# Reordering the preparation, the end of the self attention and the feed-forward weight splits of a one-core transformer block

## The chip, the core and the metric

The kernel runs on one core of a Trainium2 chip. A core has five engines with a queue each: TensorE (PE, with PEld for its weight loads), VectorE (DVE), ScalarE (ACT), GpSimd (POOL) and SyncE (SP), which here only issues DMAs. They share the on-chip memory SBUF; TensorE writes only to the eight PSUM banks. The metric is the device time of one execution in microseconds (us), the median of several runs.

## The reference

One transformer block, float32: for each of 4 batches 1024 rows of width 256, and a context of 64 rows of width 192. Sixteen heads of width 64, feed-forward width 1024.

```python
h = _ln(x, g1, be1)
x = _attn(h, h, Wq1, Wk1, Wv1, Wo1, bo1) + x          # self attention, 1024 keys
h = _ln(x, g2, be2)
x = _attn(h, context, Wq2, Wk2, Wv2, Wo2, bo2) + x    # cross attention, 64 keys
h = _ln(x, g3, be3)
y = h @ Wp + bp
a, gate = (y[..., :FF_HID], y[..., FF_HID:])
x = a * jax.nn.gelu(gate, approximate=False) @ W2 + b2 + x
```

## The kernel before

Every engine has its own function, and each is one straight program: the order of the work is the order in which the Python loops write it, and semaphores tie the engines together. A matmul operand is split into a high part and a rest (`hi`, `lo`, "split" below), and three products of parts stand for one.

**Preparation.** The context is turned and multiplied with `Wk2` and `Wv2` in 16 products (`context_product`, banks S0a, S0b, S1a, S1b, PV, PJ in turn, copied to `kv2` by DVE for even and by ACT for odd numbers). `turn_wq2` transposes `Wq2` in 16 tiles into two banks, from which ACT makes four copies to `wq2T`. DVE takes the statistics of the first batch (`stats1`), ACT the root (`ln_root`, with the load of an activation table), DVE the inverse (`ln_inverse`) and the rows `xn` of one half of the batch (`norm1`, four TENSOR_SCALAR, L684). `turn_norm` transposes `xn` (L324) through banks T0 and T1 into `hT`. `fold_keys` multiplies `wq2T` with `kv2` (L382), four times for each half of the batch. Then the query and key projections of the first head pair follow (`project_qk`, L411). POOL meanwhile splits `Wq1`, `Wk1` and `Wv1` (`split_weights`: a TENSOR_SCALAR at L1224, a TENSOR_TENSOR at L1226) and adds a bias.

**Self attention.** 64 groups C: 8 head pairs by 2 halves of queries by 4 batches. In each, TensorE makes the scores of 8 key tiles (L463, L467), ACT the exponentials, TensorE the product with the values (`attend`, L480) and the sum over the keys (`sum_keys`, L491). POOL adds up the exponentials (`add_probs`, L1273). ACT copies the sums, DVE inverts them (`invert_sums`, L782), POOL multiplies (`scale_oT`, L1279), and `out1` (L501) is the output product of a tile. For the next group DVE takes row maxima and makes `shift` (L775), without which the scores can't be finished. In the last group DVE also splits the folded keys of the cross attention (`split_keys`, L807, tile `crossA`), which `score2` needs.

**Cross attention.** A pipeline of 32 rounds i, one for each row tile: `turn2(i-2)` (transposes of the probabilities, L546), `score2(i)` (L532), `turn_half` for the next norm (in rounds with i % 4 of 2 or 3), `out2(i-3)` (L562), and in the first eight rounds `out1` of the last batch. DVE takes the inverse of each softmax sum (L817), POOL multiplies with it (`scale2`, L1284). In rounds with i % 4 of 0 or 1 DVE also makes rows `xn` (`norm2`, L684). POOL splits cross keys (L1290), cross values (L1297) and the feed-forward weights (`split_ffn`, eight pieces: `Wp` quarters, 128x1024, at even numbers and `W2` quarters, 128x512, at odd ones).

**Feed-forward.** L576 up, L590 down; the outputs are stored by SP in eight pieces of four row tiles (L1476).

Of the kernel before, what the change touches and what calls it, by code (L numbers as in the profile page):

```python
# [48 lines left out]
def block_kernel(nc, x, ctx, Wq1, Wk1, Wv1, Wo1, bo1, Wq2, Wk2, Wv2, Wo2, bo2, Wp, bp, W2, b2,  # L49
# [32 lines left out]
    with stack:  # L82
# [222 lines left out]

        def v_slot(D, jt):
            return jt

        @block.tensor
        def _(e):  # L310
# [50 lines left out]
            def turn_wq2():  # L361
                for k in range(KT):
                    for h in range(PAIRS // 4):
                        bank = f"T{(2 * k + h) % 2}"
# [233 lines left out]
            turn_wq2()  # L598
            for c in range(CHUNKS):
                turn_norm((1, c))  # L600
                for p in range(PAIRS // 2):
                    fold_keys(PAIRS // 2 * c + p)
# [26 lines left out]
            for i in range(NT + 3):  # L629
# [10 lines left out]
                if i < TILES:  # L640
                    out1(B - 1, i, ("PJ", "PV")[i % 2])
# [14 lines left out]
        def _(e):  # L656
# [122 lines left out]
            def invert_sums(C):  # L779
                need.wait_ge(s.sum_copied, C + 1)  # L780
                need.wait_ge(s.oT_scaled, C)
                e.reciprocal(inv[:, :], sums[:, :]).then_inc(s.sum_inverse, 1)  # L782
# [95 lines left out]
            for n in range(2 * PAIRS):  # L878
                context_product(n)
                if n >= PAIRS:  # L880
                    stats1(0, n - PAIRS)
            ln_inverse(rs1[:, :], (1, 0))
            for c in range(CHUNKS):
                norm1(c)
                turn_norm((1, c))
                for p in range(PAIRS // 2):
# [12 lines left out]
            for C in range(NC):  # L899
                b, n = divmod(C, BC)  # L900
                if C + 1 < NC:
# [3 lines left out]
                    gather_max(C + 1)  # L905
                if C >= 2:
                    invert_sums(C - 2)
                if b + 1 < B and 5 <= n < 5 + TILES // 2:
# [9 lines left out]
                if C == NC - 1:  # L918
                    for k in range(KT):
                        split_keys(k, 0)  # L920
                        split_keys(k, 1)
                    invert_sums(C - 1)
                whole_array(slot(C))
            for i in range(NT + 3):
# [10 lines left out]
                if i < TILES:  # L935
                    out1(B - 1, i, ("PJ", "PV")[i % 2])
                if i == 2:
                    invert_sums(NC - 1)
# [26 lines left out]
        def _(e):  # L965
# [69 lines left out]
            def turn_wq2():  # L1035
                for k in range(KT):
                    for h in range(PAIRS // 4):
                        need.wait_ge(s.wq2_turned, 2 * k + h + 1)
                        e.copy(wq2T[:, 4 * h:4 * h + 4, k * PART:(k + 1) * PART],
                               banks[f"T{(2 * k + h) % 2}"].rearrange("p (j n) -> p j n", j=4)).then_inc(s.wq2T_in, 1)  # L1040
# [52 lines left out]
            def copy_sums(C, bank="PJ"):  # L1093
                need.wait_ge(s.summed, C + 1)
                need.wait_ge(s.sum_inverse, C)
# [60 lines left out]
            ln_root(mv1[:, :, 1], (1, 0), (1, TILES - 1))  # L1156
            turn_wq2()
            for c in range(CHUNKS):
                turn_norm((1, c))
                for p in range(PAIRS // 2):  # L1160
# [58 lines left out]
        def _(e):  # L1219
# [55 lines left out]
            def scale_oT(C):  # L1275
                there = oT[:, C // CHUNKS % PRING, C % CHUNKS * BANK:(C % CHUNKS + 1) * BANK]
                need.wait_ge(s.sum_inverse, C + 1)
# [31 lines left out]

            e.memset(ident[:, :], 0.0).then_inc(s.const, 1)  # L1310
# [32 lines left out]
            for i in range(NT + 3):  # L1343
# [13 lines left out]
                if i >= TILES + 4 and i % 2 == 0 and i // 2 - TILES // 2 - 2 < 8:  # L1357
                    split_ffn(i // 2 - TILES // 2 - 2)
# [4 lines left out]
        def _(e):  # L1363
# [109 lines left out]
            for i in range(NCH):  # L1473
                b, t0 = ORDER[FORDER[i] // CHUNKS], FORDER[i] % CHUNKS * TPC
                need.wait_ge(s.y_added, TPC * (i + 1))
                e.dma_start(out[b, t0 * PART:(t0 + TPC) * PART, :].rearrange("(t p) d -> p t d", p=PART),  # L1476
                            xf[:, i % 4]).then_inc(s.y_stored, 16)
# [7 lines left out]
            need.wait_ge(s.y_stored, 16 * NCH)  # L1485
# [23 lines left out]
```

## Time and profile before

| | |
|---|---|
| median of 3 runs | 2096.39 us (2095.53 to 2096.85) |
| the profiled execution | 2095.88 us |
| its span, first to last instruction | 2094.0 us |
| TensorE matmul busy | 2060.5 us, 98% |
| VectorE / ScalarE / GpSimd busy | 1403.2 / 1044.5 / 1414.8 us |
| mean granted TensorE clock | 0.998 |

The chain of work that ended last is TensorE for 94% of the span. Preparation takes the first 60 us, self attention goes to about 1555, cross attention to about 1813, feed-forward to the end. In a row of the timeline, the bracket at the end says how long the engine was idle before the instruction and what ended that wait.

### The profile page before, as it was taken

How to read it: one execution, taken by the hardware profiler on the slowest of the kernel's cores; microseconds unless marked ns; L12 is line 12 of the kernel's file. 1: busy time of each engine (PE TensorE's matmuls, PEld its weight loads, DVE VectorE, ACT ScalarE, POOL GpSimd, SP SyncE). 2: the span in 40 equal slices, each digit the busy share in tenths (PEclk: the TensorE clock that was granted, in tenths of full speed). 3: DMA queues.
4: the chain of work that ended last, by engine and by line, in shares of the span. 5: the costliest groups of instructions: out<-in, count | busy, mean ns of one | idle time of the engine just before them, and what ended most of it. 6: DMA issues, size and time to landing. Idle time of an engine off the chain costs nothing.

```text
span 2094.0 us, 31744 instructions
## 1 busy us (share of the span) xinstructions
PE 2060.5 (98%) x12500; PEld 1401.7 (67%) x12500; DVE 1403.2 (67%) x2139; ACT 1044.5 (50%) x1644; POOL 1414.8 (68%) x745
## 2 busy tenths in 40 slices
PE   7999999999999999999999999999998999999999
PEld 5656656567556556666656666565557989888888
DVE  5667677754766875568678566757866899755453
ACT  3445456542545564345456433545655666543332
POOL 2499799975997997779799767978885577200000
PEclk9999999999999999999999999999999999999999
DMA  6400000000100000010000001000011420000100
GB/s 192 151 6 21 6 6 16 6 6 21 41 6 6 21 6 6 1 61 6 6 6 21 6 1 46 11 6 1 21 24 38 141 81 1 1 21 21 41 11 31
DMA packets 46070, 58.74 MB, mean 28 GB/s; under 512 B 5857, under 2 KB 40289, under 8 KB 44769
## 3 DMA queue, kind: packets, MB, share of 16 engines
q1 hardware_dynamic: 45920, 56.71, 8.6%
q8 instruction: 99, 1.62, 0.3%
q14 instruction: 51, 0.41, 0.1%
HBM read 38.88 MB, written 17.83 MB: 27 GB/s over the span
## 4 chain that ended last, share of the span: by engine, by line
PE 94%; DVE 2%; POOL 1%; ACT 1%; issue 1%; DMA 0%; SPq 0%; POOLq 0%; DVEq 0%; ACTq 0%
PE score L480 21%; PE score L463 17%; PE score L576 9%; PE score L467 5%; PE attn_project L590 4%; PE score L411 4%; PE attn_project L562 4%; PE score L532 4%; PE attn_project L411 4%; PE first_score L437 3%; PE attn_project L501 3%; PE score L423 3%; PE first_score L491 3%; PE attn_project L437 2%; PE score L501 2%; PE attn_project L423 1%
## 5 line engine op out<-in xcount | busy, mean ns | idle before, releaser
L1273 POOL TENSOR_TENSOR acc<-acc,pT 128x1024 f32<-128x1024 f32 x384 | 913.7, 2380 | 55.1 <-POOL acc L1273 0.4
L1080 ACT ACTIVATE pT<-score 128x1024 f32<-128x1024 f32 x512 | 524.8, 1027 | 103.9 <-PE score L467 62.0
L463 PE MATMUL score<-qk 64*128 64x512 f32 x3072 | 459.8, 399 | 4.6 <-ACT pT L1080 2.8
L480 PE MATMUL score<-pT,vT 128*64 128x512 f32 x2016 | 446.5, 595 | 0.0
L760 DVE TENSOR_REDUCE nmax<-first_score 128x1 f32<-128x512 f32 x512 | 348.3, 680 | 12.5 <-PE first_score L437 9.2
L760 DVE TENSOR_REDUCE nmax<-attn_project 128x1 f32<-128x512 f32 x512 | 347.2, 678 | 0.0
L463 PEld LDWEIGHTS score<-qk 64*128 64x128 f32 x3072 | 258.1, 184 | 126.7 <-ACT pT L1080 70.8
L480 PEld LDWEIGHTS score<-pT,vT 128*64 128x64 f32 x2016 | 139.2, 137 | 274.5 <-issue 251.8
L1270 POOL TENSOR_TENSOR acc<-pT 128x1024 f32<-128x1024 f32 x64 | 153.6, 2400 | 187.4 <-ACT pT L1080 187.4
L782 DVE RECIPROCAL inv<-sums 128x512 f32<-128x512 f32 x64 | 214.0, 3345 | 4.8 <-POOL oT L1279 4.8
L1091 ACT COPY oT<-score 128x512 f32<-128x512 f32 x63 | 36.9, 586 | 356.9 <-PE score L480 356.9
L467 PE MATMUL score<-shift,pick 64*128 64x512 f32 x1024 | 207.0, 391 | 0.0
L437 PE MATMUL first_score<-qk 64*128 64x512 f32 x512 | 200.3, 391 | 0.0
L437 PE MATMUL attn_project<-qk 64*128 64x512 f32 x512 | 200.0, 391 | 0.0
L576 PE MATMUL score<-hT,wp 128*128 128x512 f32 x768 | 183.9, 395 | 0.0
L775 DVE TENSOR_TENSOR shift<-first_score,mask 128x512 fp32r<-128x512 f32 x64 | 44.2, 691 | 191.1 <-PE first_score L447 191.1
L576 PEld LDWEIGHTS score<-hT,wp 128*128 128x128 f32 x768 | 142.4, 188 | 32.1
L1260 POOL TENSOR_TENSOR xres<-xres,rows 128x1024 f32<-128x1024 f32 x8 | 19.2, 2401 | 205.1 <-DVE xn L684 205.1
L754 DVE SCALAR_TENSOR_TENSOR qk<-score,qk 128x512 fp32r<-128x512 f32 x67 | 46.2, 690 | 153.7 <-ACT qk L1061 153.7
L1284 POOL TENSOR_TENSOR probs<-probs,rsum 128x1024 f32<-128x1024 f32 x32 | 60.9, 1905 | 90.2 <-DVE rsum L817 90.2
L467 PEld LDWEIGHTS score<-shift,pick 64*128 64x128 f32 x1024 | 100.3, 184 | 21.9 <-DVE shift L775 0.7
L1061 ACT ACTIVATE qk<-score 128x512 fp32r<-128x512 f32 x67 | 40.1, 598 | 145.1 <-PE score L411 145.1
(159 smaller groups left out, 3050.3 us busy)
## 6 DMA issues: line engine op xcount, KB each, us to landing
xres<-x_middle SPq DMA_DIRECT2D x10, 512.0 KB, 4.1
xres<-in_x SPq DMA_DIRECT2D x4, 1024.0 KB, 7.0
raw_qk<-in_L_xattn_Wq SPq DMA_DIRECT2D x32, 128.0 KB, 2.2
raw_qk<-in_L_xattn_Wk SPq DMA_DIRECT2D x32, 128.0 KB, 2.3
raw_v<-in_L_xattn_Wv SPq DMA_DIRECT2D x8, 512.0 KB, 4.1
keys_all<-keys SPq DMA_DIRECT2D x1, 4096.0 KB, 11.8
values_all<-values SPq DMA_DIRECT2D x1, 4096.0 KB, 12.4
out_x<-xres SPq DMA_DIRECT2D x8, 512.0 KB, 2.9
```

Of the source, the lines that this page charges most:

```text
L411: last = e.matmul(banks[bank], wqk[:, P % 2, w, kind, k, :], hT[:, h, k, c * BANK:(c + 1) * BANK], start=(i == k == 0), stop=(i == 2 and k ...
L437: last = e.matmul(banks[bank], qk[P % 2][r, w, q0:q0 + PART], qk[P % 2][r, 2 + h, half * BANK:(half + 1) * BANK], start=(m == 0), stop=(m ...
L463: e.matmul(bank, qk[P % 2][r, 2 + h, keys], qk[P % 2][r, w, queries], start=(part == 0), stop=False)
L467: e.matmul(bank, pick[r, :], shift[r, :], start=False, stop=True).then_inc(s.scored, 1)
L480: last = e.matmul(banks[bank][head * DH:(head + 1) * DH, :], vT[:, v_slot(D, jt), c0:c0 + DH], pT[:, jt, head, :], start=(jt == 0), stop=( ...
L501: last = e.matmul(banks[bank][:, 0:DIM], oT[:, (PAIRS * b + p) % PRING, t * PART:(t + 1) * PART], wo1[:, p, :], start=(p == 0), stop=(p == ...
L576: last = e.matmul(banks[bank], wp[q][:, w, k, which, o:o + PART], hT[:, h, k, (c % 2) * BANK:(c % 2 + 1) * BANK], start=(term == k == 0), ...
L760: e.tensor_reduce(nmax[:, head, t, half:half + 1], banks[PASS_BANKS[head][half]], AX.X, ALU.max, negate=True).then_inc(s.row_max, 1)
L782: e.reciprocal(inv[:, :], sums[:, :]).then_inc(s.sum_inverse, 1)
L1080: e.activation(pT[:, jt].rearrange("p h n -> p (h n)"), SC[R % 2][:, :], ACT.Exp).then_inc(s.exponential, 1)
L1270: e.tensor_tensor(total, pT[:, jt - 1], pT[:, jt], ALU.add).then_inc(s.probs_added, 1)
L1273: e.tensor_tensor(total, total, pT[:, jt], ALU.add).then_inc(s.probs_added, 1)
```

## The change

Six edits.

1. Preparation. TensorE turns the first half of the first norm before `Wq2`, not after; `Wq2` now goes through PV and PJ, not T0 and T1. DVE takes the statistics after context products 2 to 9, not 8 to 15. ACT makes the root after product 11, and its copies of `Wq2` stand behind the first half of the norm. DVE makes the rows of the second half before its copies of the first four folds.
2. The four key splits: one moves to the group before the last, two ahead of the inverse at the last group's start, one stays between the last two inverses.
3. The very last inverse is made in two halves, after rounds 1 and 2; `sum_inverse` counts two for each group.
4. `out1` of tile 2 goes to PV instead of PJ.
5. The eight feed-forward splits stand in rounds 14, 15, 16, 22, 23, 24, 30, 31 instead of 12, 14, ... 26.
6. The last four row tiles are stored one by one.

```diff
+        def last_out1(i):
+            return ("PJ", "PV")[(i + (i == 2)) % 2]
...
-            turn_wq2()
             for c in range(CHUNKS):
                 turn_norm((1, c))
+                if c == 0:
+                    turn_wq2()
...
-                    out1(B - 1, i, ("PJ", "PV")[i % 2])
+                    out1(B - 1, i, last_out1(i))
...
-            def invert_sums(C):
+            def invert_sums(C, halves=(0, 1)):
+                part = slice(halves[0] * BANK // 2, (halves[-1] + 1) * BANK // 2)
...
-                if n >= PAIRS:
-                    stats1(0, n - PAIRS)
+                if 2 <= n < 2 + TILES:
+                    stats1(0, n - 2)
             ln_inverse(rs1[:, :], (1, 0))
+            norm1(0)
             for c in range(CHUNKS):
-                norm1(c)
                 turn_norm((1, c))
+                if c == 0:
+                    norm1(1)
...
+                if C == NC - 1:
+                    split_keys(0, 1)
+                    split_keys(1, 0)
                 if C >= 2:
                     invert_sums(C - 2)
+                if C == NC - 2:
+                    split_keys(0, 0)
...
-                    for k in range(KT):
-                        split_keys(k, 0)
-                        split_keys(k, 1)
+                    split_keys(1, 1)
                     invert_sums(C - 1)
...
-                if i == 2:
-                    invert_sums(NC - 1)
+                if i in (1, 2):
+                    invert_sums(NC - 1, (i - 1,))
...
-            ln_root(mv1[:, :, 1], (1, 0), (1, TILES - 1))
-            turn_wq2()
+                if n == TILES + 3:
+                    ln_root(mv1[:, :, 1], (1, 0), (1, TILES - 1))
...
+            FFN_SPLITS = [i for i in range(TILES + 6, NT) if i % TILES in (6, 7, 0)]
...
-                if i >= TILES + 4 and i % 2 == 0 and i // 2 - TILES // 2 - 2 < 8:
-                    split_ffn(i // 2 - TILES // 2 - 2)
+                if i in FFN_SPLITS:
+                    split_ffn(FFN_SPLITS.index(i))
...
-                need.wait_ge(s.y_added, TPC * (i + 1))
-                e.dma_start(out[b, t0 * PART:(t0 + TPC) * PART, :].rearrange("(t p) d -> p t d", p=PART),
-                            xf[:, i % 4]).then_inc(s.y_stored, 16)
+                pieces = [slice(0, TPC)] if i + 1 < NCH else [slice(j, j + 1) for j in range(TPC)]
+                for part in pieces:
+                    need.wait_ge(s.y_added, TPC * i + part.stop)
```

The order of instructions shows the places. Rows are instructions in their engine's order, with the line of the kernel they stand in.

TensorE in the preparation, from the last context products (`ctxT,wkv`) to the first fold (`kv,wq2T`), of before:

```order
L356 MATMUL score<-ctxT,wkv 128x256 x8
L369 MATMUL first_score<-ident,wq 128x128 x16
L324 MATMUL first_score<-ident,xn 128x128 x8
L382 MATMUL score<-kv,wq2T 128x256 x8
L382 MATMUL attn_project<-kv,wq2T 128x256 x4
```

and of the change:

```order
L360 MATMUL score<-ctxT,wkv 128x256 x8
L328 MATMUL first_score<-ident,xn 128x128 x8
L373 MATMUL attn_project<-ident,wq 128x128 x16
L386 MATMUL score<-kv,wq2T 128x256 x8
L386 MATMUL attn_project<-kv,wq2T 128x256 x4
```

The 16 transposes of `Wq2` moved from ahead of the 8 transposes of `xn` to between them and the folds.

VectorE at the end of the self attention, from the last gathering of maxima to the first `score2` maximum (`nmax<-score`), of before:

```order
L767 TENSOR_REDUCE maxima<-nmax 128x2x4
L782 RECIPROCAL inv<-sums 128x512
L775 TENSOR_TENSOR shift<-first_score,mask 128x512
L782 RECIPROCAL inv<-sums 128x512
L807 TENSOR_TENSOR crossA<-crossA 128x512 x4
L782 RECIPROCAL inv<-sums 128x512
L827 TENSOR_REDUCE nmax<-score 128x16
```

and of the change:

```order
L772 TENSOR_REDUCE maxima<-nmax 128x2x4
L788 RECIPROCAL inv<-sums 128x512
L813 TENSOR_TENSOR crossA<-crossA 128x512
L780 TENSOR_TENSOR shift<-first_score,mask 128x512
L813 TENSOR_TENSOR crossA<-crossA 128x512 x2
L788 RECIPROCAL inv<-sums 128x512
L813 TENSOR_TENSOR crossA<-crossA 128x512
L788 RECIPROCAL inv<-sums 128x512
L833 TENSOR_REDUCE nmax<-score 128x16
```

Three of the four splits moved ahead of the second inverse, one of them ahead of the last `shift`.

GpSimd in rounds 12 to 16 of the cross attention (`probs` is `scale2`, `wp` and `w` are the feed-forward splits), of before:

```order
L1290 TENSOR_TENSOR crossA<-crossA 128x512 x2
L1224 TENSOR_SCALAR wp<-wp_in 128x1024
L1226 TENSOR_TENSOR wp<-wp_in,wp 128x1024
L1284 TENSOR_TENSOR probs<-probs,rsum 128x1024
L1290 TENSOR_TENSOR crossA<-crossA 128x512 x2
L1284 TENSOR_TENSOR probs<-probs,rsum 128x1024
L1254 TENSOR_TENSOR xres<-xres,rows 128x256 x2
L1224 TENSOR_SCALAR w<-w_in 128x512
L1226 TENSOR_TENSOR w<-w_in,w 128x512
```

and of the change:

```order
L1303 TENSOR_TENSOR crossA<-crossA 128x512 x2
L1297 TENSOR_TENSOR probs<-probs,rsum 128x1024
L1303 TENSOR_TENSOR crossA<-crossA 128x512 x2
L1297 TENSOR_TENSOR probs<-probs,rsum 128x1024
L1267 TENSOR_TENSOR xres<-xres,rows 128x256 x2
L1237 TENSOR_SCALAR wp<-wp_in 128x1024
L1239 TENSOR_TENSOR wp<-wp_in,wp 128x1024
L1297 TENSOR_TENSOR probs<-probs,rsum 128x1024
L1267 TENSOR_TENSOR xres<-xres,rows 128x256 x2
L1237 TENSOR_SCALAR w<-w_in 128x512
L1239 TENSOR_TENSOR w<-w_in,w 128x512
```

The `wp` split left round 12, which also holds a split of cross keys, for round 14; the `w` split went from round 14 to 15.

## Rows read from the trace of the kernel before

**Rows 1.** The page: busy time of the engines.

```profile
PE 2060.5 (98%) x12500; PEld 1401.7 (67%) x12500; DVE 1403.2 (67%) x2139; ACT 1044.5 (50%) x1644; POOL 1414.8 (68%) x745
```

**Rows 2.** Waits of TensorE: us in total, times, longest.

```profile
PE attn_project L501 <- DVE hT L714: 4.7, 2, 2.4
...
PE first_score L546 <- POOL probs L1284: 1.8, 2, 1.3
...
PE attn_project L501 <- POOL oT L1279: 1.5, 1, 1.5
...
PE score L532 <- DVE crossA L807: 1.1, 1, 1.1
```

**Rows 3.** Timeline, preparation: start, duration, engine, line, tiles, count, [idle before].

```profile
22.68 0.42 DVE L732 COPY kv<-score 128x256 f32<-128x256 f32 x1 [0.23 <-PE score L356]
...
23.34 1.04 POOL L1224 TENSOR_SCALAR wv<-raw_v 128x1024 fp32r<-128x1024 f32 x1 [3.65 <-DMA raw_v<-in_L_xattn_Wv]
...
25.43 1.05 ACT L1039 COPY wq2T<-first_score 128x512 f32<-128x512 f32 x2
...
25.80 3.59 DVE L684 TENSOR_SCALAR xn<-xres,mv,rs 128x256 f32<-128x256 f32 x4
...
27.65 1.26 POOL L1226 TENSOR_TENSOR wqk<-raw_qk,wqk 128x512 fp32r<-128x512 f32 x1
...
29.44 1.97 PE L324 MATMUL first_score<-ident,xn 128*128 128x128 f32 x8 [2.25 <-DVE xn L684]
...
30.60 0.78 ACT L1020 ACTIVATE hT<-first_score,cols 128x512 fp32r<-128x512 f32 x1 [2.78 <-PE first_score L324]
...
31.34 3.79 PE L382 MATMUL score<-kv,wq2T 64*128 64x256 f32 x16
...
37.54 1.37 DVE L684 TENSOR_SCALAR xn<-xres,mv,rs 128x256 f32<-128x256 f32 x4
...
38.97 1.10 PE L324 MATMUL first_score<-ident,xn 128*128 128x128 f32 x8 [2.09 <-DVE xn L684]
...
45.44 5.83 PE L411 MATMUL score<-hT,wqk 128*128 128x512 f32 x24 [0.15 <-DVE keys L738]
```

**Rows 4.** DMA issues, first 20 us: KB each, us from issue to landing.

```profile
xres<-in_x SPq DMA_DIRECT2D x1, 1024.0 KB, 8.2
```

**Rows 5.** Windows: us, busy time per engine, then the granted clock.

```profile
34.00:35.00 1.00, 1.00 (x8) 0.76 (x6) 1.00 (x2) 0.06 (x1) 0.00 (x0) 0.50 0.00 0
35.00:36.00 1.00, 1.00 (x12) 0.90 (x10) 0.72 (x2) 0.60 (x1) 0.00 (x0) 0.97 0.00 0
```

**Rows 6.** Timeline, end of the self attention.

```profile
1538.41 0.69 DVE L775 TENSOR_TENSOR shift<-first_score,mask 128x512 fp32r<-128x512 f32 x1 [3.21 <-PE first_score L447]
...
1543.91 3.35 DVE L782 RECIPROCAL inv<-sums 128x512 f32<-128x512 f32 x1 [4.80 <-POOL oT L1279]
...
1547.18 9.28 DVE L807 TENSOR_TENSOR crossA<-crossA 128x512 fp32r<-128x512 f32 x4
...
1561.11 3.72 PE L501 MATMUL attn_project<-wo,oT 128*128 128x256 f32 x16 [1.48 <-POOL oT L1279]
```

**Rows 7.** Timeline, TensorE, round 3 of the cross attention.

```profile
1592.59 3.72 PE L501 MATMUL attn_project<-wo,oT 128*128 128x256 f32 x16 [2.28 <-DVE hT L714]
```

**Rows 8.** Timeline, rounds 12 to 16 of the cross attention.

```profile
1671.79 3.58 DVE L684 TENSOR_SCALAR xn<-xres,mv,rs 128x256 f32<-128x256 f32 x2
...
1672.82 2.40 POOL L1226 TENSOR_TENSOR wp<-wp_in,wp 128x1024 fp32r<-128x1024 f32 x1
...
1689.01 1.90 POOL L1284 TENSOR_TENSOR probs<-probs,rsum 128x1024 f32<-128x1024 f32 x1 [0.95 <-DVE rsum L817]
...
1692.55 1.03 PE L546 MATMUL first_score<-ident,probs 128*128 128x128 f32 x8
```

**Rows 9.** The page, DMA issues over the span.

```profile
raw_qk<-in_L_xattn_Wq SPq DMA_DIRECT2D x32, 128.0 KB, 2.2
...
out_x<-xres SPq DMA_DIRECT2D x8, 512.0 KB, 2.9
```

More of the change, by code:

```diff
@@ L363, in turn_wq2 @@
                     for h in range(PAIRS // 4):
-                        bank = f"T{(2 * k + h) % 2}"
+                        bank = ("PV", "PJ")[h]
                         need.wait_ge(s.wq2_loaded, 16)
@@ L777, in make_shift @@
                                 mask[:, :].unsqueeze(2).to_broadcast([PART, TPC, PART]), ALU.mult).then_inc(s.shift_in, 1)
-            def invert_sums(C):
+            def invert_sums(C, halves=(0, 1)):
+                part = slice(halves[0] * BANK // 2, (halves[-1] + 1) * BANK // 2)
                 need.wait_ge(s.sum_copied, C + 1)
                 need.wait_ge(s.oT_scaled, C)
-                e.reciprocal(inv[:, :], sums[:, :]).then_inc(s.sum_inverse, 1)
+                e.reciprocal(inv[:, part], sums[:, part]).then_inc(s.sum_inverse, len(halves))
             def out1(b, t, bank="PJ"):
@@ L935, in _ @@
                 if i < TILES:
-                    out1(B - 1, i, ("PJ", "PV")[i % 2])
-                if i == 2:
-                    invert_sums(NC - 1)
+                    out1(B - 1, i, last_out1(i))
+                if i in (1, 2):
+                    invert_sums(NC - 1, (i - 1,))
                 if i in (TPC + 1, 2 * TPC + 1):
@@ L1039, in turn_wq2 @@
                         e.copy(wq2T[:, 4 * h:4 * h + 4, k * PART:(k + 1) * PART],
-                               banks[f"T{(2 * k + h) % 2}"].rearrange("p (j n) -> p j n", j=4)).then_inc(s.wq2T_in, 1)
+                               banks[("PV", "PJ")[h]].rearrange("p (j n) -> p j n", j=4)).then_inc(s.wq2T_in, 1)
             def fold_keys(p):
@@ L1094, in copy_sums @@
                 need.wait_ge(s.summed, C + 1)
-                need.wait_ge(s.sum_inverse, C)
+                need.wait_ge(s.sum_inverse, 2 * C)
                 e.copy(sums[:, :], banks[bank]).then_inc(s.sum_copied, 1)
@@ L1155, in _ @@
                 context_product(n)
-            ln_root(mv1[:, :, 1], (1, 0), (1, TILES - 1))
-            turn_wq2()
+                if n == TILES + 3:
+                    ln_root(mv1[:, :, 1], (1, 0), (1, TILES - 1))
             for c in range(CHUNKS):
                 turn_norm((1, c))
+                if c == 0:
+                    turn_wq2()
                 for p in range(PAIRS // 2):
@@ L1276, in scale_oT @@
                 there = oT[:, C // CHUNKS % PRING, C % CHUNKS * BANK:(C % CHUNKS + 1) * BANK]
-                need.wait_ge(s.sum_inverse, C + 1)
+                need.wait_ge(s.sum_inverse, 2 * (C + 1))
                 need.wait_ge(s.oT_written, C + 1)
@@ L1474, in _ @@
                 b, t0 = ORDER[FORDER[i] // CHUNKS], FORDER[i] % CHUNKS * TPC
-                need.wait_ge(s.y_added, TPC * (i + 1))
-                e.dma_start(out[b, t0 * PART:(t0 + TPC) * PART, :].rearrange("(t p) d -> p t d", p=PART),
-                            xf[:, i % 4]).then_inc(s.y_stored, 16)
+                pieces = [slice(0, TPC)] if i + 1 < NCH else [slice(j, j + 1) for j in range(TPC)]
+                for part in pieces:
+                    need.wait_ge(s.y_added, TPC * i + part.stop)
+                    e.dma_start(out[b, (t0 + part.start) * PART:(t0 + part.stop) * PART, :].rearrange(
+                        "(t p) d -> p t d", p=PART), xf[:, i % 4, part]).then_inc(s.y_stored, 16)
                 if i + 4 < NCH:
@@ L1484, in _ @@
             need.wait_ge(s.x2_stored, 16 * NCH // 2)
-            need.wait_ge(s.y_stored, 16 * NCH)
+            need.wait_ge(s.y_stored, 16 * (NCH + TPC - 1))
 _NAMES = ["x", "ctx_768"] + ["L0_xattn_" + n for n in (
```

## The prediction

> **What bounds the kernel now.** The page first: TensorE is busy for 2060.5 us of the 2094.0 us span [rows 1], so without taking matmuls away at most 33.5 us can be won, and the change takes none away. What counts is where TensorE stands still. The waits of TensorE come next. Of its named waits, four can be touched by the edits: 4.7 us for `hT` ahead of two `out1` tiles, 1.8 us for `probs` ahead of two `turn2`, 1.5 us for the scaled `oT` ahead of the first `out1`, 1.1 us for the key splits ahead of the first `score2` [rows 2]. Then the timeline of each of these places, to see what was late and what is late next. The preparation has further waits and also a low clock. At the very end no engine works and a store lands. Everything behind a stall of TensorE here moves as a block, since TensorE is the bound between these places; so a saving at one place should reach the end.
>
> **Preparation (edit 1).** Before, DVE is done with its context copies at 23.10 (22.68 + 0.42), then needs the root, and begins `xn` at 25.80 [rows 3]. `x` lands 8.2 us after an issue early in the stage [rows 4], so statistics between the copies hold up no copy, and the root is ready before the last copy. With about 0.25 us for the inverse `xn` can begin at 23.4, 2.4 us sooner. But the four rows took 3.59 us there, against 1.37 us for the second half [rows 3]. The difference is POOL: its four splits (`wv`, then `wqk`, two instructions each) run from 23.34, the landing of `wv`, to 28.91 (27.65 + 1.26), and `xn` ended at 29.39, just behind them. Four rows and four POOL instructions in a row: if one DVE row gets in between two POOL instructions, as the 3.58 us of the two `xn` rows against the 2.40 us `wp` split also look [rows 8], then the rows that start at 23.4, just behind `wv`'s start, are done with the last split, at 29.1. The gain is 0.3 us, not 2.4.
>
> The Trainium skill speaks against the earlier norm in the same way: SBUF — State Buffer, "Who interferes with whom", says that VectorE and GpSimd share one port pair, held by whichever starts first for its whole instruction, and that a `tensor_scalar` can be such an instruction. By that rule moving the rows earlier, into the splits, wins nearly nothing; without it the step would be worth 2.4 us and more. Here only the rows' durations bear it out.
>
> Then the path grows. Before, the `Wq2` transposes ran while DVE made `xn`; now they stand between the norm's transposes and the folds. TensorE has by then been idle for over 5 us, and restarts at the low clock: before, the granted clock was 0.50 (1.2 GHz) at 34 to 35 us and 0.97 in the next, 5.6 us after the restart at 29.44 [rows 5]. From 29.1: 8 transposes 1.97 us, to 31.1; 16 more at that rate 3.9 us. ACT first makes three activations of some 0.78 us, begun 1.16 us behind the first transpose as before, so to 32.6, and copies each quarter of `Wq2` in 0.53 us (1.05 for two) [rows 3]. Two banks hold two quarters, the third waits for the first copy (33.1), the fourth ends at 35.1, its copy at 35.6. The four folds, at the full clock again, take 32 instructions of 0.12 us (estimate: half of 3.79/16), to 39.4. The second half's rows are long there, and its transposes start at 39.4 instead of 38.97; from there to the projection at 45.44 it is the same 6.47 us. **Sum: +0.4 us.** Bounds: with no POOL in the way the rows end at 24.8, the clock stays high, and the same path ends 5.8 us sooner than before; with rows at 29.4 and the low clock through the folds (0.24 each) it is 4.6 later. If DVE's first row wins the race at 23.34 against POOL, the rows end with the third split (27.65) and the path is 2 us shorter.
>
> **End of the self attention (edits 2 to 4).** The four splits took 9.28 us, 2.32 each, from 1547.18 [rows 6], and `score2` waited 1.1 us for them [rows 2]. The inverse behind them made `out1` wait another 1.48 us [rows 6]. Now one split stands ahead of `shift`, where DVE sat idle 3.21 us: 2.32 fits. Two stand where it sat 4.80 us (1539.1 to 1543.9): 4.64 fits. The inverse (3.35), the last split (2.32) and the last inverse (3.35) then end near 1553, or 1555 if POOL comes late because DVE now gets in between its sums. TensorE needs the keys at 1555.5 and the scaled `oT` at 1558.5, and the scaling takes POOL about 1.3 us behind a sum. Both waits go: -1.1 and -1.5 us.
>
> `out1` of tile 2 waited 2.4 us for the rest of `hT`, since both used PJ [rows 2]. On PV it only needs `out1` of tile 1 added, which is long done: -2.4. In round 3 the half norm goes to PV, behind this tile's add, which DVE has made by then; `out1` of tile 3 waited 2.28 us there [rows 7] for DVE, which was late because of the whole inverse of 3.35 us in round 2. One half is now in round 1, where DVE waits for ACT's copy of the sums and delays the softmax sum by some 2 us; POOL's product for it is still done 2.7 us before `turn2(1)` by my count. So round 2 has 1.7 us less on DVE, of which 1.1 us reaches `out1`. **Sum: -1.1 - 1.5 - 2.4 - 1.1 = -6.1 us**, between -3 (only the first two, and a little) and -7.5.
>
> **Feed-forward splits (edit 5).** In round 12 the second `xn` row stood behind the `wp` split, 3.58 us for two rows, and `turn2` came 1.3 us late; in round 20 the same cost 0.5 [rows 2, 8]. Both rounds lose the split: -1.8 us. What is late next: rounds 14 and 23 now hold a product (1.9), a bias and a `wp` split (3.5), about 6.8 us of POOL in a round of 7.0. The product of the next round starts some 0.6 us late; before it ended at 1690.91 and `turn2` read it at 1692.55 [rows 8], 1.6 us of slack. Rounds 14, 15, 22 and 23 have no `xn` rows to block. In round 30 the split meets `norm3`, which delays DVE by 1.4 us; the last products have over 2 us. **-1.8 us**, between 0 and -1.8.
>
> **Stores (edit 6).** The last store of 512 KB took 2.9 us to land; a piece of 128 KB takes 2.2 (loads, the nearest row) [rows 9]. The other three leave while TensorE works. **-0.7 us**, between 0 and -1.
>
> **Sum** +0.4 - 6.1 - 1.8 - 0.7 = -8.2 us. The profiled execution took 2095.88 us, the median of the runs is 0.5 us above it. 2095.88 - 8.2 = 2087.7.
>
> **Rivals.** What a measurement of this kernel can tell from no change is 0.2%, 4.2 us.
> (a) The forecast, the late stages win and the preparation gives about nothing: 2087.7, own range 2085 to 2090. 55%.
> (b) The preparation wins too, as DVE's rows get ahead of POOL (the start at 23.4 against 23.34 is a tossed coin): 2 us or up to 5.8 us less than before instead of 0.4 more, 2081.5 to 2085.3. 25%.
> (c) The preparation costs: `Wq2` on the path at the low clock and the folds low too, +2 to +4.6: 2089.3 to 2091.9. 12%. For it speaks the longer idle of TensorE, against it that the clock rose 5.6 us after the restart.
> (d) The moves do nothing at the end of the self attention, because POOL, not DVE, is late: POOL's sums slip by each DVE instruction that gets in, and the scaled `oT` comes when it came before. Then only 2.4 + 1.8 + 0.7 are won: 2091 to 2093. 5%.
> (e) Slower: the POOL port. If each of the eight moved splits stalled `turn2` as that of round 12 did, 1.3 us each, that costs 10.4 us where nothing is won by edit 5: 2095.88 + 0.4 - 6.1 - 0.7 + 10.4 = 2099.9. It turns the sign from 0.8 us for a split on (6.4/8). Against it: eight rounds before held a split, and two waited. 3%.
>
> **How the numbers follow.** Faster by over 0.2% (below 2092.2) in (a), (b), (c) and half of (d): 0.93, less something for what I have overlooked, 0.88. Within 0.2%: 0.08. Slower: 0.04. The range goes from 2083 to 2091.5: it leaves out the far end of (b) and the ends of (c) and all beyond.
>
> **What would show it.** After: `xn` rows of the first half ending near 29 (b: near 27.7 or before), the first projection at about 45.5, a granted clock of 0.5 between; no wait of `score2` for `crossA`, none of the first `out1` for `oT`, one wait of `out1` for `hT` of about 1 us instead of 4.7 in two; no waits of L546 for `probs`; the last store 2.2 us to landing. The prediction is wrong if the first projection moves by more than 3 us, if the first splits hold up `shift`, or if new waits for `probs` appear in rounds 15, 24 or 32.

## The result, and the profile after

The changed kernel took 2082.8 us (median of 6 runs, 2082.07 to 2085.07) against 2096.39 us before (2095.53 to 2098.53): 0.9936 of the time, interval 0.9924 to 0.9949, 13.6 us less. The forecast was 2087.7, with a range from 2083.0 to 2091.5: the sign was right, the gain was 5 us larger, and the median lies 0.2 us below the range. In two later sets of runs the same kernel had medians of 2085.2 and 2084.84; why it moves so much is part of what follows.

Busy time, from the page of the changed kernel (against [rows 1]):

```profile
PE 2058.4 (99%) x12500; PEld 1400.2 (67%) x12500; DVE 1399.6 (67%) x2140; ACT 1044.2 (50%) x1644; POOL 1415.0 (68%) x745
```

The span is 2080.5 us, 13.5 less, at the same matmuls. Waits of TensorE from 1552 us, where the last attend ends, to the feed-forward part, changed kernel (against [rows 2]; total, times, longest), all that there are:

```profile
PE attn_project L566 <- ACT turned L1150: 0.8, 1, 0.8
PE first_score L550 <- ACT sums L1107: 0.8, 1, 0.8
PE attn_project L505 <- DVE hT L719: 0.7, 1, 0.7
```

No wait for `crossA`, `oT` or `probs`; of 4.7 us for `hT` 0.7 is left. Timeline of the changed kernel, preparation (against [rows 3]):

```profile
21.52 0.42 DVE L737 COPY kv<-score 128x256 f32<-128x256 f32 x1 [1.30 <-PE score L360]
...
22.09 4.26 DVE L689 TENSOR_SCALAR xn<-xres,mv,rs 128x256 f32<-128x256 f32 x4
...
22.73 1.04 POOL L1237 TENSOR_SCALAR wv<-raw_v 128x1024 fp32r<-128x1024 f32 x1 [3.80 <-DMA raw_v<-in_L_xattn_Wv]
...
23.86 2.34 POOL L1239 TENSOR_TENSOR wv<-raw_v,wv 128x1024 fp32r<-128x1024 f32 x1
...
26.41 1.25 PE L328 MATMUL first_score<-ident,xn 128*128 128x128 f32 x8 [4.06 <-DVE xn L689]
...
27.45 1.92 PE L373 MATMUL attn_project<-ident,wq 128*128 128x128 f32 x8
...
32.04 2.00 PE L386 MATMUL score<-kv,wq2T 64*128 64x256 f32 x16 [0.73 <-ACT wq2T L1050]
...
35.69 1.09 PE L328 MATMUL first_score<-ident,xn 128*128 128x128 f32 x8
...
42.16 4.19 PE L415 MATMUL score<-hT,wqk 128*128 128x512 f32 x17 [0.15 <-DVE keys L743]
```

The first projection stands at 42.16 instead of 45.44. The same view at the end of the self attention (against [rows 6, 7]):

```profile
1532.33 0.63 DVE L813 TENSOR_TENSOR crossA<-crossA 128x512 fp32r<-128x512 f32 x1
...
1536.19 4.87 DVE L813 TENSOR_TENSOR crossA<-crossA 128x512 fp32r<-128x512 f32 x2
...
1542.34 3.35 DVE L788 RECIPROCAL inv<-sums 128x512 f32<-128x512 f32 x1 [1.28 <-POOL oT L1292]
...
1545.61 2.01 DVE L813 TENSOR_TENSOR crossA<-crossA 128x512 fp32r<-128x512 f32 x1
...
1552.62 3.07 PE L536 MATMUL score<-crossA,hT 128*128 128x512 f32 x12
...
1555.53 3.61 PE L505 MATMUL attn_project<-wo,oT 128*128 128x256 f32 x16
...
1567.07 1.75 DVE L788 RECIPROCAL inv<-sums 128x256 f32<-128x256 f32 x1 [0.53 <-ACT sums L1107]
...
1582.58 3.72 PE L505 MATMUL attn_project<-wo,oT 128*128 128x256 f32 x16 [0.67 <-DVE hT L719]
```

With five landmarks of each trace the 13.5 us divide as follows:

| stretch | before | after | change | forecast |
|---|---|---|---|---|
| start to first projection | 45.44 | 42.16 | -3.28 | +0.4 |
| to the copy of the last attended heads | 1510.11 | 1510.58 | +0.47 | 0 |
| to the fourth `out1` | 37.04 | 29.84 | -7.20 | -6.1 |
| to the feed-forward part | 220.50 | 218.26 | -2.24 | -1.8 |
| to the last residual add | 277.11 | 277.11 | 0 | 0 |
| to the end of the span | 3.80 | 2.55 | -1.25 | -0.7 |

The landmarks of before are rows of [rows 3, 7], the others are in the same timelines. Most of the miss is in the first line of the table.

### The profile page after: what moved, and what is told of

The parts are those of the page before. It is cut to its first block, busy times and chain, and to the rows that moved or that the text cites. A ratio compares the mean times of both kernels' runs of the same rounds, so it can differ in the third digit from the quotient of the medians.

```text
span 2080.5 us, 31749 instructions
## 1 busy us (share of the span) xinstructions
PE 2058.4 (99%) x12500; PEld 1400.2 (67%) x12500; DVE 1399.6 (67%) x2140; ACT 1044.2 (50%) x1644; POOL 1415.0 (68%) x745
## 4 chain that ended last, share of the span: by engine, by line
PE 96%; DVE 2%; ACT 1%; issue 0%; DMA 0%; SPq 0%; DVEq 0%; ACTq 0%
PE score L484 21%; PE score L467 18%; PE score L580 9%; PE score L471 6%; PE attn_project L594 4%; PE attn_project L566 4%; PE score L536 4%; PE score L415 4%; PE first_score L441 4%; PE attn_project L415 4%; PE attn_project L505 3%; PE score L427 3%; PE first_score L495 3%; PE score L505 2%; PE attn_project L441 2%; PE attn_project L427 1%
## 5 line engine op out<-in xcount | busy, mean ns | idle before, releaser
L788 DVE RECIPROCAL inv<-sums 128x512 f32<-128x512 f32 (+1 forms) x65 | 214.7, 3303 | 3.7 <-POOL oT L1292 2.5
```

The lines of the kernel that those rows point to most:

```text
L788: e.reciprocal(inv[:, part], sums[:, part]).then_inc(s.sum_inverse, len(halves))
```

## The experiments

Ratios are to runs of the kernel before on the same chip. "Distance" below is from the start of VectorE's last `kv` copy (22.68 us before [rows 3]) to the first projection: it leaves out how early that copy comes. Its start moves between traces, from 22.52 to 23.80 us in five with the old order of the preparation and from 21.52 to 23.68 us in thirteen with the new one. TensorE's wait for the landing of `wkv` ahead of the first product is 1.4 to 3.4 us in these traces, so at least part of the scatter is that landing.

**The parts alone, and the kernel before once more.** e1: edit 1. e2: edits 2 to 4. e3: edits 5 and 6. e4: nothing changed.

> The kernel before with edit 1 alone (the preparation). Marks: start of the first projection, and the same counted from the start of the first copy of kv. Before: 45.44 and 35.57 us behind the first copy at 9.87; after the whole change: 42.16 and 33.57 behind 8.59. Theory A (landing and race): the edit itself is worth 2.0 us, because DVE gets three rows of xn in before POOL's first long instruction; the other 1.3 us is when the first weights land, which differs between executions. Then the second mark is 33.4 to 33.8, whatever the first copy's time, and the time is 2 to 3.5 us below before, ratio 0.9984 to 0.9990. Theory B (the prediction's working: one row for each POOL instruction, Wq2 on the path at the low clock): second mark 35.5 to 36.2, time as before or 0.4 us above. Theory C: the edit itself moves the first copy too, so all 3.3 us belong to it and the first copy is at 8.6 here.

> The kernel before with edits 2 to 4 alone (key splits, inverse in halves, bank of out1 tile 2). Mark: from the end of the last attend to the start of out1 of tile 3 (before 37.0 us, from 1555.55 to 1592.59; after the whole change 29.8). Theory A (the sum of four waits): 7.2 us fewer here, time 2088.5 to 2089.8. Theory B (part of that came from the shifted phase of POOL that the other edits bring): 5 us fewer or less, time above 2090.5.

> The kernel before with edits 5 and 6 alone (feed-forward splits, stores of the last rows). Marks: waits of turn2 for probs (before 1.3 and 0.5), and from the last add of the output to the end of the span (before 3.8; after 2.55). Theory A: both waits are gone and the tail is 1.25 us shorter, since a 128 KB store lands in 1.7 us and not in the 2.2 of the loads: in sum 3.0 us. Theory B: the waits went because of the other edits' phase shift, and one comes back here; 1.2 to 2.5 us in sum.

> The kernel before, unchanged, once more. Theory A (landing differs between executions): the first copy of kv starts anywhere from 8.5 to 10, and the first projection 35.6 us behind it, within 0.2. Theory C (the edit moved it): the first copy again at 9.87, within 0.1.

| run | us (runs) | beside before's | ratio, interval |
|---|---|---|---|
| e1 | 2095.81 (11) | 2096.12 (15) | 0.9995, 0.9986 to 1.0004 |
| e2 | 2088.6 (4) | 2096.12 | 0.9961, 0.9947 to 0.9974 |
| e3 | 2092.35 (1) | 2096.12 | one run |
| e4 | 2096.21 (1) | 2096.12 | one run |

e2 is worth 7.5 us and e3 3.8 in its single run (2.2 to the feed-forward part and 1.2 in the tail by its trace): theory A of both. e4 has VectorE's first `kv` copy at 8.70 us, which is theory A, but the first projection 37.3 us behind it, not 35.6: the stretch between the two scatters as well. In e1 the mark of theory A held (33.5 us) and its time did not: the trace had the first projection at 42.40, 3.0 us earlier than before, and the median stood still, in runs from 2091.25 to 2098.48. The mean granted clock of these runs goes with their time: 0.999 in the two fastest (2091.25, 2091.72), 0.998 in the next seven, 0.996 in the two slowest (2098.16, 2098.48). The trace tells where one such execution loses time. Windows of TensorE, e1 (us, busy, granted clock, DMA share, GB/s):

```profile
1574.00:1577.00 3.00, 0.55 (x3) 0.96 1.06 193
1577.00:1580.00 3.00, 3.00 (x9) 0.50 0.01 1
1580.00:1583.00 3.00, 3.00 (x19) 0.97 0.00 0
```

and the same place in the kernel before, 3 us later:

```profile
1577.00:1580.00 3.00, 0.55 (x4) 1.00 1.00 193
1580.00:1583.00 3.00, 3.00 (x16) 1.00 0.02 3
```

Both stand still for 2.45 us ahead of the third `out1`; in e1 the clock fell to 0.50 (1.2 GHz) for 3.4 us as the tile began, in the trace of before it did not. The cost is in the length of that tile (timeline, e1; 3.72 us in the kernel before):

```profile
1576.51 5.41 PE L501 MATMUL attn_project<-wo,oT 128*128 128x256 f32 x16 [2.45 <-DVE hT L715]
```

**e5: edits 1 to 4 together.** Does the preparation's gain arrive once the late waits are gone?

> Edits 1 to 4 together (preparation and end of self attention), the feed-forward splits and the stores as before. Edit 1 alone gave 2095.81 (-0.3) although its trace had the last attend 2.8 to 3 us earlier, and its clock fell to 1.2 GHz for 3.4 us at 1575 us of the span, inside the waits for the residual adds; edits 2 to 4 alone gave 2088.6 (-7.5). Theory A (the gain of edit 1 is real, 2.8 us, and was lost again to the clock in the waits at the end of self attention, which edits 2 to 4 take away): the two together give 2.8 + 7.5 = 10.3 us, 2085.8, no low clock outside the preparation, and a spread of the runs well under the 7 us of edit 1 alone. Theory B (edit 1 is worth what its own median says, the parts add up as measured): 0.3 + 7.5 = 7.8 us, 2088.3. Between them: 2087.

2087.86 us (5 runs, within 0.64) against 2095.89, ratio 0.9959 (0.9947 to 0.9972): 8.0 us less, near theory B. There was no late fall of the clock, and still edit 1 added only 0.5 us to the 7.5 of e2 (on another chip). The preparation of e5 says why, first the timeline, then windows of TensorE (us, busy, granted clock, DMA share, GB/s):

```profile
22.90 1.04 POOL L1237 TENSOR_SCALAR wv<-raw_v 128x1024 fp32r<-128x1024 f32 x1 [3.72 <-DMA raw_v<-in_L_xattn_Wv]
...
23.20 5.28 DVE L689 TENSOR_SCALAR xn<-xres,mv,rs 128x256 f32<-128x256 f32 x4
...
27.07 1.26 POOL L1239 TENSOR_TENSOR wqk<-raw_qk,wqk 128x512 fp32r<-128x512 f32 x1
```

```profile
26.00:28.00 2.00, 0.00 (x0) 0.55 1.12 324
28.00:30.00 2.00, 1.47 (x7) 0.50 0.49 25
30.00:32.00 2.00, 2.00 (x11) 0.50 0.00 0
32.00:34.00 2.00, 1.55 (x9) 0.75 0.00 0
```

GpSimd's split of `wv` began 0.3 us ahead of the first `xn` row, the four rows took 5.28 us, to just behind the end of the last split at 28.33, and the clock was low for 6.8 us. That is the forecast's own picture of this stage, with the first projection at 44.66. Which of the two engines starts first is called the race below.

**e6 to e8: two edits of the preparation in the changed kernel.** e6 puts the `Wq2` transposes ahead of the norm's again, on all engines that take part, e7 holds GpSimd back by one wait, e8 has both:

```diff
-            for c in range(CHUNKS):
-                turn_norm((1, c))
-                if c == 0:
-                    turn_wq2()
+            turn_wq2()
+            for c in range(CHUNKS):
+                turn_norm((1, c))
...
             split_wqk(0)
+            need.wait_ge(s.ln_rows, TPC)
             split_wv(0)
```

> The changed kernel, but with the Wq2 transposes ahead of the first norm's transposes again (their banks PV and PJ kept). In the trace of the changed kernel TensorE waits 4.06 us for xn (22.35 to 26.41), then does the Wq2 transposes (1.92 + 1.43 us) and waits 0.52 and 0.73 us for their copies; its clock is low from about 27 to 31 us. Theory A (the wait is only for xn, so 3.35 us of transposes fit into it): folds start at 28 instead of 32.04, VectorE's first fold copy then waits for its own xn rows (end 32.2) and not for TensorE, the first projection comes 1 us earlier through that, and 1.5 us more where the low clock is gone: 2080.3 to 2081.8. Theory B (the move of the transposes behind the norm is what won the preparation): the first projection comes 1 to 3 us later, 2084 to 2086.

> The changed kernel, but GpSimd's split of Wv waits for the first four xn rows of VectorE (one wait more on ln_rows). In the trace of the changed kernel these rows take 4.26 us (22.09 to 26.35) beside GpSimd's split, while the next four, with GpSimd idle, take 1.37 us. Theory A (the two engines hold each other up): the four rows take 1.4 us, end at 23.5, the transposes of the norm start at 23.6, and the first projection comes 2.8 us earlier, 39.3: 2080.0 (1.5 less still where the low clock goes too). GpSimd's splits then end 0.8 us later, which nothing waits for before the projection. Theory B (the rows are slow for another reason, as the DMA writes that land there): the rows take 4 us again and nothing is won, 2082.8 to 2083.6.

> Both of the last two edits in the changed kernel. TensorE does the Wq2 transposes from 22.35 to about 24.3 without a wait for xn (end 23.5), then the norm's from 24.3 and the second half of Wq2. Theory A: the idle 4.06 us are gone, the low clock of 3.4 us (1.7 us of work lost) with them, the first projection at 37.5 to 38.5 instead of 42.16: 2078 to 2079.5. Theory B (the chain through ScalarE and VectorE from the norm's transposes to the last fold copy, 15.8 us from 26.41 to 42.13, sets the projection, and only its start counts): as with GpSimd held alone, or later by the 1.9 us of Wq2 transposes that now stand ahead of the norm's where xn is early: 2080 to 2081.5.

| run | us (runs) | ratio, interval | `xn` rows | distance |
|---|---|---|---|---|
| e6 | 2082.27 (4) | 0.9931, 0.9917 to 0.9945 | 4.53 | 19.16 |
| e7 | 2079.95 (4) | 0.9922, 0.9907 to 0.9937 | 1.38 | 17.98 |
| e8 | 2082.66 (5) | 0.9933, 0.9921 to 0.9946 | 1.38 | 20.05 |

e7 came out as theory A had it (2080.0 forecast). Timeline, e7:

```profile
22.33 1.38 DVE L689 TENSOR_SCALAR xn<-xres,mv,rs 128x256 f32<-128x256 f32 x4
...
23.77 1.09 PE L328 MATMUL first_score<-ident,xn 128*128 128x128 f32 x8 [1.18 <-DVE xn L689]
...
23.80 1.04 POOL L1237 TENSOR_SCALAR wv<-raw_v 128x1024 fp32r<-128x1024 f32 x1 [4.82 <-DVE xn L689]
```

The clock stayed full throughout. In e8 my theory A (2078 to 2079.5) fell, and the time is above the range of theory B (2080 to 2081.5) too: TensorE filled the first gap with `Wq2` and the first folds, and then stood still for 4.4 us in one piece, because VectorE still had the second half's rows (3.11 us beside GpSimd) ahead of its first fold copy. The longest wait of TensorE up to 46 us, then windows, e8:

```profile
PE score L386 <- DVE keys L742: 4.4, 1, 4.4
```

```profile
30.00:32.00 2.00, 0.00 (x0) 1.00 0.00 0
32.00:34.00 2.00, 0.00 (x0) 0.76 0.00 0
34.00:36.00 2.00, 1.72 (x8) 0.50 0.00 0
```

The clock was low for 6.8 us and the gain of e7 was lost. In e6 the idle time was cut into waits of 2.1, 2.6 and 1.3 us and the clock never fell; but the rows were as long as ever. Its time lies between the two theories (2080.3 to 2081.8 and 2084 to 2086), nearer A: the full clock came, the earlier fold copies did not.

**e9 to e12: the changed kernel again, and edits 4, 3 and 2 undone one at a time.** e10 has `return ("PJ", "PV")[i % 2]` in `last_out1`, e11 one `invert_sums(NC - 1)` at `i == 2`, e12 all four `split_keys` ahead of `invert_sums(C - 1)`, as before.

> The changed kernel once more, word for word. Its preparation code is that of the kernel with edits 1 to 4 alone, whose trace had the four xn rows at 5.28 us, the clock at 1.2 GHz for 7 us and the first projection 22.03 us behind the start of VectorE's last kv copy; the first trace of the changed kernel had 4.26 us, 3.4 us and 20.64. Theory A (these differ from execution to execution, not from kernel to kernel): the distance falls anywhere from 20.4 to 22.1, the runs spread over 3 us, 2082 to 2085.5. Theory B (what the late edits do to the code shifts the preparation): 20.6 again within 0.2, 2082.3 within 0.5.

> The changed kernel with edit 4 undone: the projection of tile 2 goes to bank PJ again. Prediction's sizing: TensorE waits 2.4 us for hT ahead of it, and the wait of tile 3 stays at about 0.7, so the stretch from the first to the fourth out1 (27.05 us in the changed kernel) grows by 2.4. Rival (the bank also is what shortened tile 3's wait, since the half norm of round 3 follows tile 2's add): it grows by 3.5 to 4.0 and the wait of tile 3 is back at 2.3.

> The changed kernel with edit 3 undone: one whole inverse of 3.35 us in round 2 in place of the two halves of 1.75 us in rounds 1 and 2. Prediction's sizing: the wait of the fourth out1 grows by 1.1 us (0.67 to 1.8); the traces' sizing, 1.6 (0.67 to 2.3). Rival: the half in round 1 cost something there (VectorE's softmax sum of that round started 2.5 us later), so that undoing it gives 0.3 to 0.5 back at the third out1, net +1.2.

> The changed kernel with edit 2 undone: the four first key splits stand together ahead of the last inverse but one, 9.3 us. Prediction's sizing: the waits of the first score2 (1.1 us) and of the first out1 (1.5 us) come back, +2.6 us from the last attend to the first out1 (2.79 us in the changed kernel). Rival: with the half inverses and the other bank in place VectorE's lateness reaches further, to the softmax of tile 0 and the second out1: +3.5 to +4.5.

e9: 2085.2 us (5 runs), distance 21.47, so theory A; rows 4.80 us long, low clock for 6.8 us. The other three are read by stretches of their traces, since their medians (2088.2, 2082.57, 2086.9, of 3, 2 and 2 runs) hold the preparation's scatter too. First to fourth `out1` takes 27.05 us in the changed kernel: 29.76 in e10 (+2.71), 28.69 in e11 (+1.64). First `score2` to first `out1` takes 2.91: 4.51 in e12 (+1.60), with the 1.1 us wait for `crossA` back ahead of it. Waits of TensorE from 1540 us, e10:

```profile
PE attn_project L505 <- DVE hT L719: 3.1, 2, 2.4
```

e11:

```profile
PE attn_project L505 <- DVE hT L719: 2.3, 1, 2.3
```

e12:

```profile
PE attn_project L505 <- POOL oT L1289: 1.5, 1, 1.5
PE score L536 <- DVE crossA L813: 1.1, 1, 1.1
...
PE attn_project L505 <- DVE hT L719: 0.7, 1, 0.7
```

Each undone edit brings back its own wait and no other, and the rival of each falls (a wider reach in e10 and e12, a cost of the half inverse in round 1 in e11): 2.71 + 1.64 + 1.60 + 1.1 = 7.05 us, against 7.20 measured for the three.

By luck e11 also shows the race won: three rows began ahead of GpSimd, and the fourth took 1.13 us beside its short first instruction. Timeline, then the view by tile from 22 to 27 us (ns: min, median, max), e11:

```profile
23.17 2.10 DVE L689 TENSOR_SCALAR xn<-xres,mv,rs 128x256 f32<-128x256 f32 x4
...
24.06 1.07 POOL L1237 TENSOR_SCALAR wv<-raw_v 128x1024 fp32r<-128x1024 f32 x1 [3.80 <-DMA raw_v<-in_L_xattn_Wv]
...
L689 DVE TENSOR_SCALAR xn<-xres,mv,rs x4: 405/408/1129, 23.2 to 24.1; 128x256 f32<-128x256 f32 x4
```

**e13 to e16: with and without the race.** e13 is the kernel before with GpSimd's wait, e14 edit 1 with it, e15 and e16 the changed kernel without and with it, all on one chip.

> The kernel before, with one wait more: GpSimd's split of Wv waits until VectorE has made the first four xn rows. In its own order these rows begin 3.1 us behind VectorE's last kv copy (23.34 for GpSimd, 25.80 for VectorE) and took 3.59 us, so the race is lost there too. Theory A (the collision of the two engines is a cost by itself, whatever the order): the rows take 1.4 us, the first projection comes 2.2 us earlier (20.6 us behind the last kv copy instead of 22.8), 1.5 more where the low clock goes: 2092.5 to 2094. Theory B (the old order hides the rows' length behind the Wq2 transposes, which end at 27.2): xn then ends at 27.2 as well and is worth the same 2 us, no more; the clock stays low. What tells them apart is the clock and the distance: 19 or 20.6.

> Edit 1 and GpSimd's wait, the rest as before. If edit 1 and the wait are worth 4.8 us in the preparation (distance 18.0 instead of 22.8), and the clock still falls in the waits at the end of self attention in most runs, as with edit 1 alone: 2092 to 2094, runs spread over 4 us and more, against 2091.2 where it does not fall. Rival (the preparation's gain arrives whole): 2091.3 within 1.

> The changed kernel once more, beside the next one on the same chip. Its first two jobs gave 2082.8 and 2085.2. Expected by the race in the preparation: first projection 18.2 to 22.0 us behind the last kv copy, by whether xn begins ahead of GpSimd's split of Wv; runs from 2082 to 2085.8.

> The changed kernel with GpSimd's wait once more, beside the changed kernel. Theory A (the wait takes the race out): 2.5 to 4 us below the kernel of the run before this one, the rows at 1.38 us again, full clock all through the preparation, and a spread below 1.5 us. Rival (its 2079.95 was a lucky chip): the same time as the changed kernel within 1 us.

| run | us (runs) | ratio, interval | distance |
|---|---|---|---|
| e13 | 2095.69 (10) | 0.9996, 0.9986 to 1.0005 | 21.31 |
| e14 | 2093.72 (10) | 0.9985, 0.9976 to 0.9995 | 18.00 |
| e15 | 2084.84 (4) | 0.9945, 0.9930 to 0.9960 | 20.76 |
| e16 | 2081.59 (4) | 0.9929, 0.9914 to 0.9944 | 17.99 |

Side by side the wait is worth 3.25 us (e15 to e16), theory A, and the distance repeats to 0.02 us in e7, e14 and e16. In the old order its median shows no gain (e13), against the 2092.5 to 2094 of theory A. The rows took 1.38 us too, but TensorE's clock was low afterwards for 6.8 us, and the distance is 21.31, above the 20.6 that was expected with a low clock. It is still 1.5 us less than before, and the trace gives that back at the third `out1`, as e1 does. Timeline, e13:

```profile
1578.71 5.41 PE L501 MATMUL attn_project<-wo,oT 128*128 128x256 f32 x16 [2.45 <-DVE hT L714]
```

e14 loses time there too, in its trace twice. Timeline, e14:

```profile
1575.37 5.41 PE L501 MATMUL attn_project<-wo,oT 128*128 128x256 f32 x16 [2.45 <-DVE hT L715]
...
1590.05 5.21 PE L501 MATMUL attn_project<-wo,oT 128*128 128x256 f32 x16 [2.28 <-DVE hT L715]
```

The two tiles are 1.7 and 1.5 us longer than at the full clock (3.72). Of its ten runs five lie at 2092.4 to 2093.4 us with a mean granted clock of 0.999 and five at 2094.1 to 2094.7 with 0.998. The median is in the expected range; the spread, 2.3 us, is less than the 4 us that were expected, and no run came near 2091.2.

## Why the prediction was right in sign and off in size

**Preparation: the step that failed.** "Then the rows that start at 23.4, just behind `wv`'s start, are done with the last split, at 29.1" took one outcome of a race for the forecast, although rival (b) called it a tossed coin. The first projection moved by 3.28 us, beyond the 3 us that the prediction set as its sign of being wrong, and the rows ended at 26.35, not near 29. The start itself was well placed: the rows begin 0.57 us behind the last `kv` copy (0.7 forecast). The picture of one row for each GpSimd instruction was right as well. In the changed kernel two of the four rows had begun when GpSimd started at 22.73. The third began with it and took 1.2 us (the median of 0.80 below is the mean of 0.41 and 1.18), and the fourth took 2.5 us, from 23.8 to 26.35, just behind the end of GpSimd's long instruction at 26.20. The view by tile, changed kernel, from 21 to 27 us (durations in ns: min, median, max):

```profile
L689 DVE TENSOR_SCALAR xn<-xres,mv,rs x4: 406/797/2506, 22.1 to 23.8; 128x256 f32<-128x256 f32 x4
```

What the coin costs is seen across the traces, by who started first:

| trace | `xn` ahead of `wv` by | four rows | TensorE idle | low clock | distance |
|---|---|---|---|---|---|
| e7, e14, e16 | held | 1.38 | 1.2 | none | 18.0 |
| e11 | 0.89 | 2.10 | 1.9 | none | 18.2 |
| changed kernel | 0.64 | 4.26 | 4.1 | 3.4 | 20.6 |
| e12 | 0.38 | 4.61 | 4.4 | 3.4 | 20.9 |
| e1, e10, e15 | 0.19 to 0.33 | 4.51 to 4.58 | 4.3 to 4.4 | 3.4 | 20.8 to 20.9 |
| e5 | -0.30 | 5.28 | 5.1 | 6.8 | 22.0 |
| e9 | -1.12 | 4.80 | 4.6 | 6.8 | 21.5 |
| before | -2.46 | 3.59 | 2.2 | 6.8 | 22.8 |

Two more traces with the old order, e3 and e4, have distances of 23.0 and 23.5, and e2, old order too, with rows of 2.84 us and 3.4 us of low clock, 21.1. Against the 22.8 of the kernel before, the new order is worth 0.7 and 1.3 us where VectorE loses (e5, e9), about 2 where it starts a little ahead, and 4.6 where it starts 0.9 us ahead. What counts is how many rows begin ahead of GpSimd: with one or two a row still meets the 2.34 us instruction, with three none does. The forecast's +0.4 is the case lost, sized about 1 us too dear by e5: half of it on the way through `Wq2` to the folds (6.5 us forecast from the norm's transposes, 6.0 in e5), half in rows that it had end at 29.1. The profiled execution had it at -3.28: 2.1 from the distance, 1.2 from `kv` copies that came earlier, which by the scatter told above need not be the change's.

The Trainium skill, SBUF — State Buffer, "Who interferes with whom", has whoever issues first hold the port pair for its whole instruction. The 2.5 us of the fourth row beside the 2.34 us GpSimd instruction agree, and so do 1.38 us with GpSimd held. The rule was right; using it as a reason for no gain was not, since it also says that the one who comes first wins.

The measured 2082.8 lies in the range of rival (b), 2081.5 to 2085.3, and its reason is seen in the trace. But (b) had the late stages at 8.6 us as the forecast did, where they measured 10.7, so that number is partly luck. Rival (c) needs a first projection 2 us later than before, and no trace with the new order has a longer distance than before; (e) needs `probs` waits, and there are none. Two figures of the prediction don't follow from its own: rows that end at 27.65 instead of 29.1 shorten the path by 1.45 us, not 2, and the chances of faster add up to 0.55 + 0.25 + 0.12 + 0.025 = 0.945, not 0.93.

**Where the preparation's gain went when alone.** e1, e13 and e14 have it in their traces and lose part of it to the clock at the third or fourth `out1`. The prediction did not look there for the clock: it took "a saving at one place should reach the end" for granted. With edits 2 to 4 the 2.45 us wait is gone and 2.28 has become 0.67; none of the traces with them has a low clock there. An estimate of what then arrives: e16 and e7 lie 14.9 and 15.9 us below the kernel before beside them; less 10.7 us for the late stages, measured below, that leaves 4.2 and 5.2 us for edit 1 with GpSimd's wait, which alone gave 2.8 (e14). Why the same wait is followed by a fall in some executions and not in others stays open: the traces of before, e3 and e4 have both waits at the full clock, and so has e10 with the one and e11 with the other.

**End of the self attention.** Three of the four waits went and the fourth shrank, as forecast; the term was mis-sized: 7.2 us instead of 6.1. The bank is worth 2.71 instead of 2.4, more than the wait of 2.45 itself: without a wait the tile is also shorter (3.61 instead of 3.72) and begins before the last matmul ahead of it has ended. The split inverse is worth 1.64 instead of 1.1, nearly all of the 1.7 us that it takes off VectorE in round 2, and the splits 2.7 instead of 2.6. Rival (d) fell: GpSimd's scaling begins at 1553.52, ahead of the first `out1` by 2 us.

**Feed-forward splits.** -2.24 instead of -1.8: both `probs` waits are gone, and each gave back 0.2 us more than its own length, as the bank's did. From the last `out2` product to `score2` TensorE took 3.25 us in round 12 and 2.48 in round 20 (waits of 1.28 and 0.52), against 1.75 without a wait: 1.50 + 0.73 = 2.23 us. The expected late product in round 30 (`xn` rows of 2.03 us beside a split) made nobody wait.

**Stores.** -1.25 instead of -0.7. The four pieces landed in 1.7 us (median), against the 2.2 that the loads suggested; the view of DMA issues, changed kernel (against [rows 9]):

```profile
out_x<-xres SPq DMA_DIRECT2D x4, 128.0 KB, 1.7
```

**Sum.** Errors of 3.7 - 0.5 (given back in the main loop) + 1.1 + 0.4 + 0.5 make 5.2 us; the profiled execution of 2082.31 lies 5.4 below the forecast. The 0.5 us of the main loop is missing in the traces of edit 1 alone and of edits 2 to 4 alone (1510.09 and 1510.13 us from the first projection to the copy of the last heads). It is there, at 1510.34 to 1510.64, in all traces that have edit 1 together with two or three of edits 2 to 4; its cause stays open. The late stages alone would have given 2096.39 - 10.7 = 2085.7 by their measured terms, inside rival (a)'s own range. The best version found is the changed kernel with GpSimd's wait: 2079.95 and 2081.59 us in two sets of runs.

## What to carry to other kernels

Where two engines that block each other are released close together, one of them by a landing (here GpSimd, by that of `raw_v`), do not forecast one outcome: price both, and if one line of waiting can fix the order, put it in; it was worth 3.3 us here, and the stretch then repeated to 0.02 us. Read the granted clock beside every wait of TensorE that an edit lengthens, joins or moves: e6, with its idle time in three pieces of 2.6 us at most, kept the full clock where e8, with one of 4.4 us, lost it for 6.8 us. And before adding up gains, check that the waits left downstream do not take them back; here the same edit and wait were worth 2.8 us with the late waits in place and, by estimate, 4.2 to 5.2 without them.

## What the runs showed of the hardware that was not expected

The low stretches of TensorE's clock, always at 0.50 (1.2 GHz), came in two lengths. In the preparation they lasted 3.4 us (changed kernel, e1, e2, e10, e12, e15) or 6.8 us (before, e3, e4, e5, e8, e9, e13), at the late `out1` tiles 3.4 us (e1, e13, e14 twice), and once begun they went on while TensorE was busy again. No length of wait below 4 us divides the cases. Behind the context products all eight idle stretches of over 4 us came with one. Of those between 2.1 and 2.6 us some did (before, e3 and e13 in the preparation, the third `out1` in e1, e13 and e14) and others did not (e6, the third `out1` in before, e3, e4 and e10), and in e2 the fall came behind two of 1.7 and 1.5 us.

Four rows of 128x256 on VectorE took 1.38 us alone and up to 5.28 us beside GpSimd's splits, one row being let through for each GpSimd instruction. Beside one of 2.34 us a row that takes 0.41 us alone took 2.5 us (changed kernel, e1, e5, e9, e12): here the short instruction paid the long one's length.
